# Gated cross attention and mixture of experts: values and router ahead of the projection's unit in the first half of each step

## The reference, cut to what matters

```python
Qh = (q @ Wq + bq)...;  Kh = (k @ Wk + bk)...;  Vh = (v @ Wv + bv)...
scores = einsum('bqhd,bkhd->bhqk', Qh, Kh) / sqrt(10.0)
scores = where(mask == 0, -1e9, scores)
out = einsum('bhqk,bkhd->bqhd', softmax(scores), Vh)
x = x + tanh(g_xattn) * out
# then: scores of 8 experts on layernorm(x), top 1024 tokens of each, silu(x W1) * (x W3) W2, weighted, added
```

## Time and profile before

| | before |
|---|---|
| median of 3 runs | 811.61 us (811.11 to 812.39) |
| profiled execution | 812.18 us |
| its span | 810.3 us |
| mean granted TensorE clock | 0.967 |
| TensorE busy (share of the span) | 751.2 us (93%) |
| TensorE weight load | 630.0 us (78%) |
| VectorE | 563.0 us (69%) |
| ScalarE | 513.0 us (63%) |
| GpSimd | 365.2 us (45%) |

### The profile page before, as it was taken

The page is one execution under the profiler, slowest core; times in us unless marked ns, Lnnn a source line. Parts: engine busy times, 40 slices in busy tenths (PEclk is TensorE's granted clock), DMA queues, the critical chain, the costliest instruction groups (busy, mean ns, idle before and its releaser), DMA issues. The chain is left out here.

```text
span 810.3 us, 24962 instructions
## 1 busy us (share of the span) xinstructions
PE 751.2 (93%) x9638; PEld 630.0 (78%) x9638; DVE 563.0 (69%) x1451; ACT 513.0 (63%) x1001; POOL 365.2 (45%) x760
## 2 busy tenths in 40 slices
PE   9999999999999999999998712899999999999994
PEld 5778888888888888888886511788989898898984
DVE  7777788778877887788768698685654846465340
ACT  4366777777777777777766675556555555656532
POOL 5324453445344534453423230737456384846605
PEclk9999999999999999999999855999999999999998
DMA  7444434553355346534332270544536364524404
GB/s 231 127 128 141 148 118 126 187 175 123 120 188 174 105 139 189 173 114 129 126 109 84 81 215 20 170 112 88 112 73 126 87 124 123 85 38 80 46 8 53
DMA packets 76773, 97.08 MB, mean 120 GB/s; under 512 B 8264, under 2 KB 55880, under 8 KB 76616
## 3 DMA queue, kind: packets, MB, share of 16 engines
q1 hardware_dynamic: 63120, 77.52, 29.8%
q0 software_dynamic: 12288, 17.05, 12.9%
q10 hardware_dynamic: 1248, 0.92, 0.3%
HBM read 52.37 MB, written 25.72 MB: 96 GB/s over the span
## 5 line engine op out<-in xcount | busy, mean ns | idle before, releaser
L750 DVE TENSOR_REDUCE m_sb<-a_ps 128x4 f32<-128x512 f32 x256 | 164.2, 683 | 52.4 <-PE a_ps L1063 50.8
L572 ACT ACTIVATE p_t<-b_ps 128x512 f32<-128x512 f32 x252 | 141.8, 589 | 67.3 <-PE b_ps L1071 64.8
L1063 PE MATMUL a_ps<-k_st,q_st 31*128 31x128 f32 x2048 | 148.6, 282 | 6.7 <-DVE m_sb L750 2.7
L1487 POOL DMA_INDIRECT out<-y,idx_add x64 | 100.4, 1569 | 113.5 <-ACT y L1548 86.8
L1063 PEld LDWEIGHTS a_ps<-k_st,q_st 31*128 31x128 f32 x2048 | 124.8, 186 | 31.6 <-issue 21.9
L1071 PE MATMUL b_ps<-q_st,k_st 32*128 32x128 f32 x1984 | 143.8, 283 | 0.0
L484 POOL TENSOR_TENSOR x<-o_n,x_res 128x256 f32<-128x256 f32 x63 | 46.2, 733 | 186.6 <-DVE o_n L840 167.8
L1071 PEld LDWEIGHTS b_ps<-q_st,k_st 32*128 32x128 f32 x1984 | 120.2, 186 | 0.0
L1749 DVE TENSOR_TENSOR act_h<-act_h,bank 128x512 f32<-128x512 f32 x64 | 44.0, 687 | 83.0 <-PE bank L1892 79.9
L1892 PE MATMUL bank<-x_hi,w_hi 128*128 128x512 f32 x248 | 97.6, 394 | 0.6 <-ACT act_h L1536 0.6
L1892 PE MATMUL bank<-x_lo,w_hi 128*128 128x512 f32 x248 | 96.6, 390 | 0.0
(11 more groups left out here) (305 smaller groups left out, 1738.2 us busy)
## 6 DMA issues: line engine op xcount, KB each, us to landing
w<-in_w_t SPq DMA_DIRECT2D x24, 512.0 KB, 5.0
rows_scratch<-xg SPq DMA_DIRECT2D x16, 528.0 KB, 3.5
x_in<-in_x SPq DMA_DIRECT2D x16, 512.0 KB, 4.8
c_t<-in_ctx_t SPq DMA_DIRECT2D x16, 512.0 KB, 4.3
k_st<-k_val SPq DMA_DIRECT2D x64, 128.0 KB
q_st<-q_val SPq DMA_DIRECT2D x64, 128.0 KB, 2.4
x_res<-in_x SPq DMA_DIRECT2D x16, 512.0 KB, 3.9
out<-x SPq DMA_DIRECT2D x16, 512.0 KB, 3.5
```

Of the source, the lines that this page charges most:

```text
L572: act.activation(p_t[b.s % 2][:, 4 * r:4 * r + 4, :], ps[q % 2][:].rearrange("p (h s) -> p h s", s=P), ACT.Exp, scale=SCALE).then_inc(exp_ ...
L750: dve.tensor_reduce(m_sb[b.s % 2][:, 4 * q:4 * q + 4], a_ps[q % 2][:].rearrange("p (h s) -> p h s", s=P), AX_X, ALU.max).then_inc(max_done, 1)
L1063: mm = pe.matmul(a_ps[i][:, t * P:(t + 1) * P], q_st[p][r:r + A_K, t, tok], k_st[p][r:r + A_K, t, tok], start=True, stop=True)
L1487: pool.indirect_dma_start(out[:, :], bass.IndirectOffsetOnAxis(ap=idx_add[e % 2][:, st:st + 1], axis=0), y[st][:], None, compute_op=ALU.ad ...
```

## The change

In the first half of a step the values, and at j = 1 the router, are issued before the projection's unit. Nothing is added or removed, and no wait is changed; the lists of the other engines stay as they are.

```diff
                 scores(b, 0)
                 max_t(b)
+                for q in range(4):
+                    values(b.back(3), q, g.on(-3))
+                if b.j == 1:
+                    router(g.on(-3), b)
                 if not first(g):
                     front(g.on(1), 2 * b.j + 1)
                 elif b.j < 3:
                     front(g.on(1), 2 * b.j + 2)
-                for q in range(4):
-                    values(b.back(3), q, g.on(-3))
-                if b.j == 1:
-                    router(g.on(-3), b)
                 scores(b, 1)
```

## The result

| | before | after |
|---|---|---|
| median | 811.61 us (811.11 to 812.39, 3 runs) | 849.41 us (849.31 to 851.82, 3 runs) |
| ratio | | 1.0471 (1.0456 to 1.0485) |
| profiled execution, its span | 812.18, 810.3 | 851.82, 850.1 |
| mean granted clock | 0.967 | 0.967 |

The change costs 37.8 us; 851.5 was forecast, in a range of 834 to 858.

The account below looks back on a forecast made before the run. Each step's loop was taken to close over VectorE, which takes the unit out before its small block and second maxima. 14 groups x 2.85 = 39.9 us on the median 811.6 gave 851.5 us, range 834 to 858.

Parts of the forecast that it names:

- The sum: Groups 1 to 14: four steps' costs of 1.01, 0.61, 0.77 and 0.46 make 2.85 us a group, 39.9 us in all.
- Tilings: Each step: values start 0.21 us behind the narrow transposition where the unit started 0.03 behind, 0.18 us more a step.
- j = 3: Step j = 3: late unit 7 delays VectorE's small block and second maxima; step 6.44 to 7.45 us, +1.01.
- j = 0: Step j = 0: late unit 1 delays its copy, remainder and VectorE's block; step 6.32 to 6.93 us, +0.61.
- j = 1: Step j = 1: values and router precede unit 3, so keys and second maxima come later; 7.40 to 8.17 us, +0.77.
- the wait for unit 2: Step j = 0: unit 2 waits for its bank until 4.47 us, due 4.04; TensorE's own list then gives 6.93 us.
- j = 2: Step j = 2: ScalarE takes unit 5 out, so no new loop wait; tiling 0.18 plus knock-on 0.28, +0.46 us.
- the wait of the transposition: At j = 2 the maxima's transposition waits for VectorE's copy of the router's turned scores from j = 1: +0.28 us.
- The reading that pointed to VectorE: In 330 us the scores' weight load waited 14 times for a maximum, 0.21 us each, about once a group.
- That only the tilings cost: Rival (a), whole attention: the late unit is absorbed and 10 us of tiling remain, 821.7 us; chance 0.11.
- the narrow pieces run together without a switch: Rival (c): transposition, values and router run without emptying the array, 0.22 us less in 56 steps, 799.3 us; chance 0.03.
- Neutrality by a full TensorE: Rival (b): the sum of TensorE's work is the same and no wait bites, 811.6 us; chance 0.04.

Follow-up runs that it names:

- the pair of kernels that differ in it: Kernel before with values ahead of the unit at j = 2 alone, 814.72 us; the same with the narrow transposition also behind the values, 812.99 us.

## Why the prediction was right

*The sum.* 39.9 us were forecast for the 14 groups and 36.9 came in the trace, 2.85 against 2.63 a group on average; the rest of the measured 37.8 is within the scatter of the runs. Nearly all the errors made the forecast too long; the largest are named below.

*Tilings.* Values 0.21 us behind the narrow transposition and unit 1.01 behind the values are as forecast (249.45, 249.66, 250.67). The price, 0.18 a step, is shown by the pair of kernels that differ in it: 379.6 against 376.8 us in the 14 groups of their traces, 0.20 a group, and 0.17 within the half step shown. Their medians, 2.65 against 0.62 us over the runs of before, would make it 0.15, because of the last group of the second.

*j = 3.* Forecast 4.04, 4.71, 5.95, 7.45 for unit taken out, block, maxima, next step; the trace has 4.04, 4.71, 5.96, 7.45. Shown as the cause by turning the block and the unit round. One wait I had not seen: `out_back` wants the scaled result, which is now late too (0.40 us of TensorE's idle time, at 254.44). By the rows it costs nothing: the transpositions behind it start at 254.94, the next step could follow 0.53 later at 255.47, and it starts at 255.80, behind the maxima.

*j = 0 and j = 1.* The mechanism held and the size was a little off, in one term: the time from VectorE's last write to TensorE's next start. I had taken 0.21 us for it from one place, the start of j = 0. It is that there, after the change too (254.31 + 1.28 = 255.59, start 255.80). But at the start of j = 2 it is 0.05 (269.32 + 1.28 = 270.60, start 270.65), and for unit 2, 0.06 (259.44 + 0.69 = 260.13, start 260.19). At j = 0 the wait for unit 2 decides; 0.15 us less there, against a remainder of unit 1 that is made 0.07 later than I had it (copy at 258.81, 3.01 after the step's start, and remainder 0.63 behind it), gives the 6.86 instead of 6.93. At j = 1 the same term is 0.16 of the 0.18 by which 8.17 was too long. No run takes the wait of unit 2 away; that it decides at j = 0 is read from the trace, and from the kernel with the block in front, which leaves the step at 6.86. The step behind it, j = 1, therefore starts without a wait for the maxima: TensorE waits for line 750 at the start of two of four steps, not of three as forecast.

*j = 2.* Forecast +0.46, measured +0.51 in the group shown; the wait of the transposition is 0.30 (242.36 - 240.96 less 1.10). It is real, since moving the copy ahead gives 3.85 us back, 3.2 by the traces. The forecast counted it in 14 groups; it stands in 11 (11 x 0.30 = 3.3), which is 0.8 us of what the sum had too much.

*The reading that pointed to VectorE.* The 14 waits of the earlier trace rows were weaker evidence than I took them for. 13 of them stand at the start of j = 1 and are 0.19 us long on average, and at the starts of j = 2 and 3, where nothing is waited for, the same weight load shows 0.17. The place on which the forecast rests, the start of j = 0, is booked as "issue" in the kernel before too. That the conclusion was right is owed to the timelines of the earlier trace rows, not to this table.

*The rivals.* That only the tilings cost would have left 27.8 us a group. That the narrow pieces run together without a switch, the case of a faster kernel, fails on the same 0.21. Neutrality by a full TensorE fails too: that it showed a product in flight for 99.77 of 100 us did not keep it from being held up when a result that others wait for came later. The loop closes over VectorE, which has a fifth of its time free. The Trainium skill, Perfetto Trace Analysis, Identifying the Most-Contended Engine, names the engine with the highest occupancy as the one to optimise and warns that matmul busy time doesn't tell how close TensorE is to its limit. By weight load too TensorE comes first here (83.46 against VectorE's 79.92 us), so no share of busy time foretold that its order mattered. Which engine a faster version of the kernel before would have to relieve, no run here shows.

## What to carry to other kernels

When two pieces of work change places on a busy engine, their sum says nothing: ask for each who takes its result, and what stands behind that in the taker's own queue. The piece whose result another in-order engine waits for goes first, and independent work of the taker goes ahead of its wait, not behind it; here 1.24 us of small operations behind the wait were worth some 22 us in the kernel. Pieces that use the array in the same tiling should stand side by side, at 0.17 us for each switch saved.

## What I had not expected

The time from VectorE's last write to TensorE's start is not one number: 0.21 us at each start of j = 0 in three kernels (before, after, and with the block first, where 185.10 + 1.29 = 186.39 and the start is 186.60), 0.05 to 0.06 at two other places. The trace shows a difference between the places. At the start of j = 0 TensorE's sequencer executes a wait instruction of its own ahead of the first weight load, in all three kernels; here in the kernel after, between 255.5 and 255.8:

```profile
L138 PEldq EVENT_SEMAPHORE x1: 51/51/51, 255.7 to 255.7; - x1
```

It starts 0.10 us behind the end of the maxima, and the first product 0.11 behind its start. At 260.19 and 270.65 none stands between. `scores` waits for two counts more at j = 0, the spread queries and keys, and this fits; no kernel without them was run, so the cause is not shown.
